# The attention scores of a decoder block: one product for k_hi against q_hi and q_lo, and a sum of two halves behind it

## What is computed

```python
q = apply_rope(rmsnorm(q, q_norm_w), cos, sin)     # 16 heads of 128
k = apply_rope(rmsnorm(k, k_norm_w), cos, sin)
scores = jnp.einsum('bhtd,bhsd->bhts', q, k) * scale
scores = 50.0 * jnp.tanh(scores / 50.0)
scores = jnp.where(mask[None, None], -jnp.inf, scores)
attn = softmax(scores)
out = jnp.einsum('bhts,bhsd->bhtd', attn, v)
```

## Time and profile before

| | |
|---|---|
| three runs, median | 2057.85 us |
| the profiled execution, its own time | 2063.05 us |
| its span in the profile | 2061.3 us |
| PE busy | 1993.2 us (97%) |
| VectorE busy (DVE) | 1073.2 us (52%) |
| ScalarE busy (ACT) | 922.6 us (45%) |
| GpSimd busy (POOL) | 1013.0 us (49%) |
| score products L1037 | 768 |
| tanh L1245 | 256, 363 ns at the median |

### The profile page before, as it was taken

One profiled execution on the slowest core, in us unless ns is written; L12 is line 12 of the kernel. 1 busy time (PEld: TensorE's weight loads), 2 busy tenths in 40 slices (PEclk: granted clock), 3 DMA queues, 4 the chain that ended last, 5 costly groups with the idle time before them and its releaser, 6 DMA issues.

```text
span 2061.3 us, 40646 instructions
## 1 busy us (share of the span) xinstructions
PE 1993.2 (97%) x12136; PEld 1804.6 (88%) x12137; DVE 1073.2 (52%) x2351; ACT 922.6 (45%) x2119; POOL 1013.0 (49%) x1076
## 2 busy tenths in 40 slices
PE   6999999999999999999878999899999999999998
PEld 5888888888888888888768899799999999999997
DVE  4765555555667766777666655333333333333332
ACT  4655555554565666657555412233333333233232
POOL 5444444442344444444556206666733333488885
PEclk9999999999999999999989999999999999999999
DMA  9677777777877868777635237666643343499899
GB/s 319 222 235 247 257 249 251 246 245 274 299 257 270 324 238 316 269 264 280 215 95 186 93 102 264 226 205 212 230 137 121 121 127 125 133 214 222 192 215 244
DMA packets 188986, 450.48 MB, mean 219 GB/s; under 512 B 21696, under 2 KB 21952, under 8 KB 188864
## 3 DMA queue, kind: packets, MB, share of 16 engines
q1 hardware_dynamic: 135392, 338.68, 47.8%
q0 software_dynamic: 21504, 51.13, 10.5%
q10 hardware_dynamic: 31968, 59.12, 8.9%
HBM read 275.36 MB, written 173.48 MB: 218 GB/s over the span
## 4 chain that ended last, share of the span: by engine, by line
PE 89%; DMA 3%; POOL 2%; DVE 2%; issue 2%; ACT 1%; SPq 1%; ACTq 0%; POOLq 0%
PE bank L1125 21%; PE bank L976 16%; PE bank L1135 11%; PE bank L1027 8%; PE bank L1001 8%; PE bank L166 6%; PE bank L579 5%; PE bank L1013 4%; PE bank L1037 4%; PE bank L589 3%; PE bank L596 2%; PE bank L1049 1%; DMA xT<-xT_att 1%; DMA raw<-in_weights 1%; POOL w_lo L177 1%
## 5 line engine op out<-in xcount | busy, mean ns | idle before, releaser
L1125 PE MATMUL bank<-w_hi,xT 128*128 x1776 | 473.8, 329 | 2.1 <-DVE xT L1713 2.1
L976 PE MATMUL bank<-w_hi,xT 128*128 128x512 f32 x1024 | 354.3, 407 | 5.0 <-DMA xT<-xT_att 3.5
L1408 POOL TENSOR_TENSOR rr<-rr,expo 128x4 f32<-128x4 f32 x128 | 128.9, 1007 | 423.7 <-DVE rr L1606 423.7
L606 DVE TENSOR_TENSOR hT<-bank,hT 128x384 fp32r<-128x384 f32 x143 | 79.7, 558 | 475.1 <-ACT hT L603 475.1
L1125 PEld LDWEIGHTS bank<-w_hi,xT 128*128 128x128 f32 x1776 | 315.9, 188 | 9.4 <-issue 4.0
L1125 PE MATMUL bank<-w_lo,xT 128*128 x888 | 286.4, 323 | 0.0
L976 PEld LDWEIGHTS bank<-w_hi,xT 128*128 128x128 f32 x1024 | 195.4, 191 | 45.8 <-issue 5.3
L1135 PE MATMUL bank<-w_hi,hT 128*128 x666 | 229.9, 399 | 2.7 <-DVE hT L606 2.5
L603 ACT ACTIVATE hT<-bank 128x384 fp32r<-128x384 f32 x143 | 70.2, 491 | 329.6 <-PE bank L596 315.7
L1001 PE MATMUL bank<-w_hi,xT 128*128 128x256 f32 x1024 | 214.7, 293 | 0.0
L976 PE MATMUL bank<-w_lo,xT 128*128 128x512 f32 x512 | 202.1, 395 | 0.0
(11 more groups left out here) (242 smaller groups left out, 4432.6 us busy)
## 6 DMA issues: line engine op xcount, KB each, us to landing
xT<-xT_att SPq DMA_DIRECT2D x126, 512.0 KB, 5.2
w_hi<-w_split SPq DMA_DIRECT2D x64, 512.0 KB, 6.7
w_lo<-w_split SPq DMA_DIRECT2D x64, 512.0 KB, 7.7
xg<-blank SPq DMA_DIRECT2D x111, 264.0 KB, 4.7
yg<-blank SPq DMA_DIRECT2D x111, 256.0 KB, 5.9
raw<-in_weights SPq DMA_DIRECT2D x82, 272.0 KB, 3.1
w_split<-w_hi SPq DMA_DIRECT2D x64, 272.0 KB, 3.4
w_split<-w_lo SPq DMA_DIRECT2D x64, 272.0 KB, 3.7
```

The costliest lines, as they stand in the source:

```text
L976: last = pe.matmul(bank[par][:, :], xT[:, par, a, c * P:(c + 1) * P], w_hl[w][:, fw, c * 512:(c + 1) * 512], start=n == 0, stop=n == 11)
L1125: last = pe.matmul(out_[:, 0:I], xT[:, par, a, c * P:(c + 1) * P], flat(w_hl[w])[:, bass.ds(at + (c * 2 * I + half_ * I), I)], start=n == ...
L1408: pool.tensor_tensor(rr[:, :], rr[:, :], expo[:, :], ALU.pow).then_inc(pw_done, 1)
```

## The change

The q operand of the scores is now q_hi and q_lo of a head side by side, so that k_hi meets both in one product of 256 columns. The second product, k_lo by q_hi, adds to the first 128 of them. Each head now has 256 columns in S_ and the whole bank is used: a head's first half holds hi by hi and lo by hi, its second half hi by lo. ScalarE copies the second halves to th, VectorE adds the first halves to th, and tanh reads th in SBUF. The oT copy moves from behind exp to between ScalarE's copy and tanh. In VectorE's list the addition stands between L1634 and the low part of oT. TensorE's next write of S_ waits for the addition instead of tanh. The layernorm statistics count on one semaphore instead of two.

```diff
-            dve.tensor_scalar(nmean[:, slot, :], mv[:, slot, :, 0], -1.0, None, ALU.mult).then_inc(mean_done, 1)
+            dve.tensor_scalar(nmean[:, slot, :], mv[:, slot, :, 0], -1.0, None, ALU.mult).then_inc(var_done, 1)
...
-            pool.wait_ge(var_done, k + 1)
+            pool.wait_ge(var_done, 2 * k + 2)
             pool.tensor_tensor(rstd[:, slot, :], rstd[:, slot, :], expo[:, 0:2], ALU.pow).then_inc(rstd_done, 1)
-            pool.wait_ge(mean_done, k + 1)
...
                         pe.wait_ge(qkT_hi, s)
                         pe.wait_ge(qkT_lo, s)
-                        wait(pe, th_done, 2 * s - 2)
+                        wait(pe, s_sum, 2 * s - 2)
                         for h in range(HG):
-                            for n, (a, w) in enumerate(TERMS):
-                                last = pe.matmul(S_[:, h * T:(h + 1) * T], qkT[:, a, (HG + h) * T:(HG + h + 1) * T],
-                                                 qkT[:, w, h * T:(h + 1) * T], start=n == 0, stop=n == 2)
+                            k_of, at = slice((HG + h) * T, (HG + h + 1) * T), 2 * h * T
+                            pe.matmul(S_[:, at:at + 2 * T], qkT[:, 0, k_of], qkT[:, :, h * T:(h + 1) * T],
+                                      start=True, stop=False)
+                            last = pe.matmul(S_[:, at:at + T], qkT[:, 1, k_of], qkT[:, 0, h * T:(h + 1) * T],
+                                             start=False, stop=True)
                         last.then_inc(s_done, 1)
...
                     if mid:
                         act.wait_ge(s_done, s)
+                        wait(act, ex_done, s - 1)
+                        act.activation(heads(th), S_[:, :].rearrange("p (h a n) -> p h a n", h=HG, a=2)[:, :, 1, :],
+                                       ACT.Copy).then_inc(s_sum, 1)
+                    if back:
+                        act.wait_ge(ot_done, s - 1)
+                        act.activation(oT[:, 0, :, :], heads(OT_[:, 0:256]), ACT.Copy).then_inc(oT_hi, 1)
+                    if mid:
+                        act.wait_ge(s_sum, 2 * s)
                         act.wait_ge(rms_done, s)
                         for h in range(HG):
-                            act.activation(th[:, h * T:(h + 1) * T], S_[:, h * T:(h + 1) * T], ACT.Tanh,
+                            act.activation(th[:, h * T:(h + 1) * T], th[:, h * T:(h + 1) * T], ACT.Tanh,
                                            scale=rk[:, 1 - par, h:h + 1]).then_inc(th_done, 1)
                         act.wait_ge(th_done, 2 * s)
                         wait(act, p_lo, s - 1)
                         act.activation(ex, th, ACT.Exp, scale=CAP).then_inc(ex_done, 1)
-                    if back:
-                        act.wait_ge(ot_done, s - 1)
-                        act.activation(oT[:, 0, :, :], heads(OT_[:, 0:256]), ACT.Copy).then_inc(oT_hi, 1)
...
                         dve.tensor_tensor(xres[:, bb, :], xres[:, bb, :], Y_[:, :], ALU.add).then_inc(acc_done, 1)
+                    if mid:
+                        dve.wait_ge(s_sum, 2 * s - 1)
+                        dve.tensor_tensor(heads(th), S_[:, :].rearrange("p (h a n) -> p h a n", h=HG, a=2)[:, :, 0, :],
+                                          heads(th), ALU.add).then_inc(s_sum, 1)
                     if back:
                         dve.wait_ge(oT_hi, s - 1)
```

More of the change, by code:

```diff
@@ L133, in build @@
         stats_done, aggr_done, rstd_done, ln_done = sem("stats_done"), sem("aggr_done"), sem("rstd_done"), sem("ln_done")
-        var_done, mean_done, nm_done = sem("var_done"), sem("mean_done"), sem("nm_done")
+        var_done, nm_done, s_sum = sem("var_done"), sem("nm_done"), sem("s_sum")
         xg_zero = sem("xg_zero")
```

## The result

The changed kernel takes 2064.85 us (median of 13 runs, 2061.34 to 2067.95) beside 2060.64 us of the kernel before in the same rounds (13 runs, 2056.27 to 2062.09): a ratio of 1.0023, 95% interval 1.0014 to 1.0031. It is slower, by some 4 us.

A forecast was written before the change was run, and what follows sets the result against it. PE was taken to bound attention's first half, and mostly the second. Terms -13.2 + 3 + 15 + 1.5 = +6.3 us, carried over to the median of 2057.85, gave 2064 us; the range for 8 in 10 was 2038 to 2085.

The forecast's parts named there:

- PE's saving, -0.21 a step: Scores of each attention step: two of six weight loads go, -0.21 us a step, bounds 0 and -0.25.
- The rival by which columns count: Scores: a product costs its columns, so PE saves nothing and the first half stands still; 2077 us, chance 0.06.
- The first half, -13.2: Attention's first 64 steps: PE's saving stands in full, 63 steps x 0.21 = -13.2 us.
- has no gap: First half of attention: one step, read as lasting 7.55 us, leaves PE no wait.
- The chain in the first half: First half: tanh starts 0.94 us after L976, pT 2.87, sq 3.19, and PE's work covers it.
- The ring, +3 over the half: Second half: through VectorE's program order, sq of one step gates tanh of the next; some +3 us.
- Collisions, 15 of at most 18: Second half: GpSimd's mask falls behind VectorE operations that cannot run beside it; 15 us taken, bounds 0 and 18.
- The drain, +1.5: Last attention steps: nothing covers the longer chain; 0.75 to 0.9 us more, twice, +1.5.
- The clock as a rival: Second half: ten PE waits growing to about 2 us lower its clock; about 2084 us, chance 0.14.

The follow-up runs named there:

- the third lot: Last of three lots of experiment runs, with both kernels measured again: changed kernel at ratio 1.0019, kernel before at 2061.79 us.
- The version with the addition first: Changed kernel with VectorE's addition moved ahead of rot and the xres addition: 2164.65 us beside 2137.08, ratio 1.0122.

## Why the prediction was right, and where not

Slower, 2064.0 forecast and 2064.85 measured. That the two figures lie so close is in part luck: the forecast added +6.3 us to a median of three runs, 2057.85, and the median of thirteen is 2060.64, so the difference is +4.2 (+2.2 between the two profiles). The mechanisms, a cheaper score block in the first half and ring and collisions in the second, are the ones that were found. The terms:

- **PE's saving, -0.21 a step.** Measured -0.235 (7.31 for 7.55). The score block is 0.42 for 0.62, and splitting the wide product again gave 0.62 back. A narrow product costs its weight load. The rival by which columns count is out: it would have left the first half at 7.55 us. The Trainium skill (TensorE: Matmul & The Clock Gate, section Back-to-back issue gap) gives the rule that I used for a product by itself, and says in the same section that it under-counts narrow products that each need a weight load, with about 81 ns for 128 columns; I had left that out. The trace agrees with the rule where no load is waited for (0.06 between 393.18 and 393.24) and with the second statement in kind, but at 0.11 us here.
- **The first half, -13.2.** Measured -11.1. What failed is "has no gap": I read one step and took all 63 for it. The last step of each group of eight already waited for GpSimd's last weight piece (7.86 us for 7.55), and the new chain makes that piece 0.19 later: 8.05. Such a step loses 0.19 instead of winning 0.235; six of them cost 6 x 0.425 = 2.6 of the 63 x 0.235 = 14.8. Another 1.2 is missing in the first twelve steps (step 12 at 119.39 for 121.02), but the same code reaches step 12 between 117.5 and 120.9 in other runs, so that figure says little. Making the piece early takes 0.74 off each of the six steps, 4.4 us, and with that also what the kernel before lost there.
- **The chain in the first half.** Tanh at 0.93 (0.94 forecast), pT at 2.92 (2.87), sq at 3.24 (3.19), nothing of it on the path: right.
- **The ring, +3 over the half.** Tanh at 1.59 after L975 in slot 9, as worked out. With the mask taken out of its way slot 9 still was 1.1 above the kernel before (forecast +1.0): 0.66 of that goes when the addition stands ahead of rot and xres, 0.43 is the longer chain. Slots 7 and 8 take 7.92 and 7.93, where the ring was to make them 7.87. In slot 6 it was oversized, 7.51 for 7.87: behind the long step of slot 5 the ring is still open there, and tanh starts at 0.82 to 1.32. From slot 7 on it starts at 1.58 to 1.59 in most turns. Of slots 1 to 5, which were to keep their saving of 0.21, slots 2, 3 and 4 did. Slot 1 kept 0.05: it takes 9.91 with narrow products, so PE's saving is there, and the chain takes most of it back.
- **Collisions, 15 of at most 18.** The kind was right; sizes and places were not. Slot 9: 0.66 and not 0.95, since L526 was well on its way when the mask came (677.08, with L526 from 676.66 to 677.88). Slot 0: 0.36. In slots 7 and 8, where 0.4 each was forecast, nothing was lost: the mask starts with 0.21 of the scan left and takes its usual time, in all twelve steps.

```profile
668.13 1.23 DVE L517 TENSOR_TENSOR_SCAN pS<-a,e2v 128x516 f32<-128x516 f32 x1
669.27 1.69 DVE L522 TENSOR_TENSOR qS<-qS,aA 128x1024 f32<-128x1024 f32 x1
```

```profile
669.14 0.74 POOL L1428 TENSOR_TENSOR ex<-ex,mask 128x256 f32<-128x256 f32 x1 [2.49 <-ACT ex L1258]
```

In slot 2 the mask does collide, 1.82 us instead of 0.74, but no step is longer for it: 7.74. In slot 1, where I had not looked, it falls behind L489 and takes 1.40. Slot 5 was put at +0.24 a turn and lost 1.0 on average over five turns (9.85 for 8.85): the wait for pT grew from 1.4 to 1.9, and in two turns the clock fell (below). Ring and collisions were forecast at 18 together; from step 65 to 127 the loss is 13.6.
- **The drain, +1.5.** The last two waits for pT were 1.95 and 0.78 and are 2.13 and 1.70. From the start of step 127 to the end of attention's last product it takes 0.8 us more (26.6 for 25.8, and the same 0.8 in the third lot). The kind was right, the size too large. The stages behind attention took 1.0 less in this profile and the same as before in the third lot, so that part is noise.
- **The clock as a rival.** It did not fall in slots 9 and 0 as I had feared (granted 1.00 from 674.27 to 684.29 and from 691.84 to 701.58), but it did fall in slot 5, where I had not looked (below).

The forecast's total came out nearer than its parts. Against the profiles, where +6.3 stands beside +2.2, there were 2.1 us too much gain in the first half, 4.4 too much loss in the second, and 1.7 behind step 127.

## What to carry to other kernels

A product that waits for its weights costs its load: send more columns through the same weights, and check what then has to be added outside. If the partial results must be summed on other engines, look where that sum stands in their program order, because everything ahead of it there becomes a condition of what follows: here sq of one step began to gate tanh of the next. Where engines are idle in one stage and busy in the next, such a trade can be made in the first alone: here that is all of the gain, and mixing slot by slot in the second added nothing. And a shorter step with a longer chain finds the next producer that was just in time, so look at the odd steps of a period too, not at one typical step.

## What was not expected of the hardware

**Equal waits, different clocks.** Slot 5 comes in two lengths, 9.45 and 11.02 us, in the same kernel. Both begin alike: pT is late by the collision with the scan L493 (the mask takes 2.57 to 2.74 us), and PE waits. The changed kernel, timeline and busy time of the stretch:

```profile
740.81 0.86 PE L1012 MATMUL bank<-vE,pT 128*128 128x130 f32 x6 [1.91 <-issue]
```

```profile
739.30:743.50 4.20, 2.69 (x18) 2.46 (x19) 3.87 (x14) 2.81 (x7) 1.30 (x3) 1.00 1.02 414
```

The version with the addition first:

```profile
761.31 1.50 PE L1012 MATMUL bank<-vE,pT 128*128 128x130 f32 x6 [1.89 <-issue]
```

```profile
760.00:765.60 5.60, 4.29 (x19) 3.84 (x19) 3.36 (x12) 2.61 (x7) 2.90 (x3) 0.70 1.02 407
```

PE waited 1.91 us and stayed at the full clock in one, waited 1.89 and ran on at a granted clock of 0.70 on average in the other, that is, for the larger part at 1.2 GHz instead of 2.4: the six products of L1012 take 1.50 us instead of 0.86. The step costs 1.6 us more. The kernel before, whose wait there is 1.4 us, shows no slot 5 above 9.2 in five turns; the changed one shows 10.3 and 11.0 in two turns of five in its first profile and 10.2 and 11.0 in the third lot; in the version with the addition first it was four of five. Over these turns in all profiles, the clock fell in 17 of the 39 with a wait of 1.60 to 1.92 us for pT, and in none of the 23 with a wait of 1.07 to 1.42. What decides among the 39, the runs don't tell.

**The later one waits.** I had read the earlier trace rows as a mask that is slowed down by VectorE. Put side by side, the cases say more. The mask that fell behind L526 ended at 678.48, 0.60 after L526's end; in slot 5 of the changed kernel it ended 0.53 after the scan:

```profile
735.66 3.05 DVE L493 TENSOR_TENSOR_SCAN qS<-a,e 128x1032 f32<-128x1032 f32 x1
```

```profile
734.13 2.42 POOL L457 TENSOR_TENSOR dE<-kS,oS 128x1024 f32<-128x1024 f32 x1
736.67 2.57 POOL L1428 TENSOR_TENSOR ex<-ex,mask 128x256 f32<-128x256 f32 x1
```

In both, as in the earlier trace rows (0.59), most of the 0.74 us of the mask's own work came after VectorE was through. The scan itself had started 0.89 us before GpSimd's L457 ended, and took 3.05 us instead of the 2.38 to 2.42 of the kernel before, where in slot 5 the mask came first, in 0.73 us. In slot 8 above it is VectorE's L522 that comes second: it starts with 0.61 of the mask left and takes 1.69 instead of the 1.19 of the kernel before. So the second one loses, whichever engine it is. The price of a collision is what is left of the first operation when the second begins, less 0.1 to 0.25 us that the second does get done, and not a fixed sum for a pair of operations. In slot 9 the mask began with 0.80 us of L526 left (677.08, end at 677.88) and lost 0.66; the forecast had 0.95 left and nothing done. With 0.21 left, in slots 7 and 8, it lost nothing.
